# A transformer block with adaptive layer norm and routed experts: batch normalisation of six batches moved from ScalarE to GpSimd, clearing of Q moved from GpSimd to ScalarE, modulation rows spread out

## The reference, cut to what matters

```
mod = silu(c) @ wmod                      # sa, ca, ga, sb, cb, gb for each batch
ga, gb = sign * max(|.|, 0.25)
h = layernorm(x) * (1 + ca) + sa
x = x + ga * attention(h)                 # softmax over 512 keys, 16 heads, 8 batches
h = layernorm(x) * (1 + cb) + sb
x = x + gb * experts(h)                   # top 2 of 8 experts by router logits, gelu between two layers
```

## Time and profile before

| | us |
|---|---|
| median of 3 runs | 657.2 (657.08 to 659.72) |
| the profiled execution's own time | 659.18 |
| its span, first to last instruction | 657.3 |
| front, up to the first maximum on DVE | 52.6 |
| opening, up to the first exponential | 77.3 |
| loop, up to the last exponential | 466.4 |

### The profile page before, as it was taken

The page is one execution under the profiler, slowest core; times in us unless marked ns, Lnnn a source line. Parts: engine busy times, 40 slices in busy tenths (PEclk is TensorE's granted clock), DMA queues, the critical chain, the costliest instruction groups (busy, mean ns, idle before and its releaser), DMA issues.

```text
span 657.3 us, 18907 instructions
## 1 busy us (share of the span) xinstructions
PE 571.7 (87%) x6699; PEld 309.7 (47%) x6699; DVE 499.3 (76%) x1134; ACT 435.2 (66%) x767; POOL 326.2 (50%) x566
## 2 busy tenths in 40 slices
PE   2667999999999999999999999997899687799970
PEld 2321243343443343343343343342589686799970
DVE  4777999989788788788788788787657375565597
ACT  2552488888778788778778778777744353456771
POOL 4444101034456656656656665655065546455571
PEclk9787999999999999999999999999998898899995
DMA  7872400220210310211210220101232122232545
GB/s 199 305 230 91 120 8 11 52 51 11 73 30 25 81 38 26 79 37 26 73 44 24 59 62 19 33 11 38 48 84 58 53 58 75 66 84 70 167 149 168
DMA packets 49867, 48.23 MB, mean 73 GB/s; under 512 B 15616, under 2 KB 44336, under 8 KB 49056
## 3 DMA queue, kind: packets, MB, share of 16 engines
q1 hardware_dynamic: 42256, 36.27, 20.5%
q0 software_dynamic: 4320, 8.92, 4.3%
q10 hardware_dynamic: 3200, 1.84, 1.0%
HBM read 28.77 MB, written 16.53 MB: 69 GB/s over the span
## 4 chain that ended last, share of the span: by engine, by line
PE 67%; DVE 16%; issue 5%; ACT 4%; another core or an unknown queue 3%; POOL 1%; DMA 1%; DVEq 0%; POOLq 0%; SPq 0%; ACTq 0%
PE ps L1018 16%; PE ps L1059 15%; PE ps L1049 13%; DVE neg_max L1363 10%; PE ps L1127 8%; PE ps L1138 7%; ACT P L1226 2%; PE ps L1086 1%; DVE P L275 1%; PE ps L1101 1%; ACT parts L1282 1%; PE ps L1037 1%; DVE ln_stats L259 1%; PE ps L1118 1%
## 5 line engine op out<-in xcount | busy, mean ns | idle before, releaser
L1363 DVE TENSOR_REDUCE neg_max<-ps 128x1 f32<-128x512 f32 x512 | 320.3, 683 | 65.3 <-PE ps L1018 60.4
L1226 ACT ACTIVATE P<-ps,zero 128x1024 f32<-128x1024 f32 x256 | 272.8, 1112 | 80.4 <-PE ps L1049 79.9
L1018 PE MATMUL ps<-K,Q 128*32 128x512 bf16 x2048 | 186.9, 385 | 7.1 <-DVE neg_max L1363 5.0
L1049 PE MATMUL ps<-Q,K 128*32 128x512 bf16 x2048 | 155.4, 380 | 8.6 <-issue 5.2
L1059 PE MATMUL ps<-P,V 128*32 128x512 f32 x1024 | 133.1, 594 | 1.6 <-ACT P L1226 1.4
L1018 PEld LDWEIGHTS ps<-K,Q 128*32 128x32 bf16 x2048 | 54.0, 95 | 127.3 <-DVE neg_max L1363 78.7
L1575 POOL DMA_INDIRECT y_rows<-P,to_now x71 | 70.9, 999 | 86.0 <-DVE P L1415 51.8
L1282 ACT ACTIVATE parts<-ps,parts 128x128 f32<-128x128 f32 x228 | 64.0, 379 | 60.6 <-PE ps L1127 26.7
L1049 PEld LDWEIGHTS ps<-Q,K 128*32 128x32 bf16 x2048 | 50.7, 96 | 74.1 <-issue 34.2
L773 POOL DMA_INDIRECT h_sorted<-diag,slot x64 | 64.4, 1007 | 28.6 <-POOL max_parts L79 13.4
L1127 PE MATMUL ps<-parts 128*128 128x128 f32 x456 | 64.7, 285 | 8.4 <-issue 6.7
(11 more groups left out here) (231 smaller groups left out, 602.2 us busy)
## 6 DMA issues: line engine op xcount, KB each, us to landing
Q<-q_parts SPq DMA_DIRECT2D x24, 384.0 KB
xs<-h_sorted SPq DMA_DIRECT2D x71, 65.0 KB
W<-w_t SPq DMA_DIRECT2D x2, 2048.0 KB, 10.9
q_parts<-parts SPq DMA_DIRECT2D x8, 384.0 KB, 3.0
Q<-y_rows SPq DMA_DIRECT2D x6, 512.0 KB, 4.5
diag<-att_u SPq DMA_DIRECT2D x128, 16.0 KB
Q<-max_parts SPq DMA_DIRECT2D x96, 4.0 KB
out<-Q SPq DMA_DIRECT2D x6, 256.0 KB, 2.3
```

Of the source, the lines that this page charges most:

```text
L1018: ins = eng.matmul(ring_bank(*unit)[QUAD * q:QUAD * (q + 1), :], Q[buffer_of(g)][:, g % NG * G + j, at:at + QUAD], K[buffer_of(g)][:, 0, : ...
L1049: ins = eng.matmul(bank(2 * u + j)[QUAD * q:QUAD * (q + 1), :], K[p][:, 1, at:at + QUAD], Q[p][:, g % NG * G + 2 * u + j, :], start=True, ...
L1226: nc.scalar.activation(P[s % 2][:, 2 * u:2 * u + 2, :], bank(2 * u, 2).rearrange("p (j t) -> p j t", j=2), ACT.Exp, bias=zero[:], scale=SC ...
L1363: eng.tensor_reduce(neg_max[g % 2][:, j * T + s:j * T + s + 1], ring_bank("maximum", g, s, j), AX.X, ALU.max, negate=True).then_inc(ring_u ...
```

## The change

1. `normalize_rows` on ACT goes. `normalized`, four `tensor_scalar` on POOL, stands behind `newton_root` in the group before (n = 2), for batches 0 to 5. Batches 6 and 7 stay on DVE.
2. On POOL `route(…, 1)` moves behind `rows`, next to `route(…, 2)`; `route(…, 3)` stays ahead of `top_two`.
3. ACT clears Q[0] (behind its first activation) and Q[1] (behind its part of the front), each in two Copy activations of 128x2048 words; POOL's two memsets go, and the wait between them.
4. The modulation rows stand after every third unit from unit 5 on; ACT reads out the first maxima after four of them instead of before all.

```diff
 def prepare_gpsimd(eng):
     for operand in (rw, K[0], K[1]):
         eng.memset(operand[:].bitcast(I32), 0).then_inc(op_set, 1)
-    eng.wait_ge(silu_done, START + 1)
-    eng.memset(Q[0][:].bitcast(I32), 0).then_inc(op_set, 1)
...
         normalize(eng, b, xn_done, ON_POOL)
-    eng.memset(Q[1][:].bitcast(I32), 0).then_inc(op_set, 1)
...
 def prepare_scalar(eng):
+    def clear(p):
+        for half in halves_of(Q[p]):
+            nc.scalar.activation(half, zero[:].to_broadcast(list(half.shape)), ACT.Copy).then_inc(cleared, 1)
...
     nc.scalar.activation(silu_den[:], cT[:], ACT.Exp, bias=zero[:], scale=-1.0).then_inc(silu_exp, 1)
+    clear(0)
...
+    clear(1)
...
+def normalized(eng, b):
+    eng.wait_ge(rstd2_own, START + (b + 1) * NEWTON_OPS)
+    if b >= 2:
+        eng.wait_ge(rows_own, START + (b - 1) * ROWS_OPS)
+    for n in range(b * T, (b + 1) * T):
+        eng.tensor_scalar(xn2[b % 2][:, n - b * T, :], X[:, n, :], rstd2[:, n:n + 1], shift2[:, n:n + 1],
+                          ALU.mult, ALU.add).then_inc(xn2_done, 1)
...
-                        b = g * (G * T) + n - 12
-                        if b >= 0 and b % 2 == 0 and b // 2 < B:
-                            modulation_row(b // 2)
+                        b = g * (G * T) + n - 5
+                        if b >= 0 and b % 3 == 0 and b // 3 < B:
+                            modulation_row(b // 3)
...
-                maxima_out(0)
                 for b in range(B):
+                    if b == 4:
+                        maxima_out(0)
...
-                            if s == 0 and u == 1 and batch_at(g, 3) in IN_LOOP:
-                                normalize_rows(batch_at(g, 3), (0, 1))
-                            if s == 1 and u == 0 and batch_at(g, 3) in IN_LOOP:
-                                normalize_rows(batch_at(g, 3), (2, 3))
...
                     if batch_at(g, 2) in IN_LOOP:
                         variance(eng, batch_at(g, 2))
                         newton_root(eng, batch_at(g, 2))
-                    if batch_at(g, 7) in EARLY:
-                        route(eng, batch_at(g, 7), 1)
+                        normalized(eng, batch_at(g, 2))
                     if batch_at(g, 3) in IN_LOOP:
                         rows(eng, batch_at(g, 3))
                     if batch_at(g, 7) in EARLY:
+                        route(eng, batch_at(g, 7), 1)
                         route(eng, batch_at(g, 7), 2)
```

29 lines of the change are left out of this document (9 added, 20 removed).

## The result

| | before | changed |
|---|---|---|
| median of 16 runs each, us | 659.02 (655.4 to 662.47) | 654.92 (652.99 to 657.78) |
| ratio, with its 95% interval | | 0.9944 [0.9928, 0.9961] |
| span of the profiled execution | 657.3 | 653.6 |
| first maximum on DVE | 52.59 | 48.24 |
| first exponential on ACT | 77.32 | 71.85 |

The change is faster by 2.6 to 4.7 us (0.4 to 0.7%), not by 8.6. The forecast had the direction right and the size wrong; 654.9 lies above the range of 644.0 to 653.2. A part of that is the starting point: the forecast stood on 657.2, the median of three runs, and sixteen gave 659.02. In the gain, 4.1 us by the medians, the change fell short of 8.6 by more than half. The two profiled executions differ by 3.64 us, and I follow that number through the stages.

The account below looks back on a forecast made before the run. PE bounds the loop's plain groups, DVE paces the opening, POOL's memset stalls the front. 4.9 - 0.2 + 1.4 + 5.0 - 2.5 = 8.6 us off the 657.2 median gives 648.6; own range 646 to 651.5, whole range 644.0 to 653.2.

Parts of the forecast that it names:

- front: Front: without POOL's memset of Q[1] the 7.88 us step becomes 2.93; gain taken as 4.9 us.
- clearing of Q[0]: Ahead of ACT's copy of mod_T: idle time hides the clearing but for 0 to 0.7 us; 0.2 taken.
- opening: Opening: spread modulation rows cut DVE's waits for PE; gain 1.4 us with one slow row, ends -1.8 and +3.0.
- normalisation: Loop: PE no longer waits behind ACT's normalisation, 0.84 us in each of six groups, 5.0 us gained.
- scatters: Groups 11, 15, 19, 23, 27: scatter stalls take back 0.5 us each, 2.5 in all; ends 0 and 6.5.
- the gain moves to the scatters: Rival, loop: four scatters in a row stall ACT each time, costing 6.5 us instead of 2.5, so 652.6; 15%.
- the wait for a store that I had as a rival: Rival, front: a store or batch 0's load hides the gain, 1 us instead of 4.9, so 652.5; 8%.
- the rival of a POOL that shuts DVE's maxima out: Rival, loop: POOL's new instructions hold up DVE's maxima, 2.5 us in six groups, 15 us, so 663.6; 4%.
- All known costs at their worst: Whole kernel: the worst ends of all terms together give -0.5 us, or 657.7.

Follow-up runs that it names:

- e8: The changed kernel with the normalisation of the first six batches back on ACT, on a free chip: 621.1 us, ratio 0.9908 to the kernel before.
- e5: The changed kernel itself, run again on a free chip: 615.15 us, ratio 0.9806 to the kernel before.
- e1: The kernel before with only the clearing of Q[0] and Q[1] moved to ACT, on a free chip: 622.7 us, ratio 0.9934.
- e13: The changed kernel with one pair of scatters in each of four groups, on a stalled chip: 653.07 us, ratio 0.9910 to the kernel before.
- e3: The kernel before with only the normalisation moved to POOL, second scatter pair still ahead of the rows, on a free chip: 630.2 us, ratio 1.0055.
- e4: The changed kernel with only the second scatter pair put back ahead of the rows, on a free chip: 624.2 us, ratio 0.9955 to the kernel before.
- e16: The changed kernel itself, run a third time, on a stalled chip: 654.98 us, ratio 0.9943 to the kernel before.
- e12: The changed kernel with scatters and plain DMAs added in plain 10.78 us groups, stalled chip: two scatters in a row 11.88 us, four 14.41, plain DMAs 10.78.
- e7: The changed kernel with two or four scatters and plain DMAs added in plain groups, on a free chip: those groups stay at 10.78 us.
- e15: The changed kernel with scatters added singly, spaced by POOL sums, or four narrow in a row, stalled chip: groups of 10.94, 10.91 (two), 11.49 (four), 14.05 us.
- e9: The changed kernel with group 10's scatter pair moved ahead of group 12's, likewise for each early batch, on a stalled chip: 665.9 us, ratio 1.0105 to before.
- e6: The changed kernel with the first four batches' scatters a group later, the fifth's eight together in group 28, on a free chip: 635.5 us, ratio 1.0126 to before.
- e2: The kernel before with only the modulation rows spread, on a free chip: 627.0 us, ratio 1.0015.
- e14: The changed kernel with a batch's eight scatters one by one, other POOL work between them, on a stalled chip: 645.03 us, ratio 0.9796 to before.

## Why the prediction was wrong, step by step

| term | forecast | measured |
|---|---|---|
| front | +4.9 (3.5 to 4.95) | +4.35 in the pair of traces; +5.5 as the mean of sixteen traces with the clearing on ACT (48.4) against four without (54.0) |
| clearing of Q[0] | -0.2 | 0.0 |
| opening | +1.4 (-1.8 to +3.0) | +1.12; +1.2 as a mean |
| normalisation | +5.0, 6 x 0.84 | +5.6, 6 x 0.94 (group 7 here; e8 against e5) |
| scatters | -2.5 (-6.5 to 0) | -6.4 on stalled chips (groups 10 to 28), 0 on free ones |
| not forecast: clock in group 30 | 0 | -1.6 in this pair |
| the rest of the trace | 0 | +0.5 |

**The step that failed is the fifth, the price of the scatters.** I took 0.5 us for each of five groups. In groups 10 to 28 the scatters cost 239.1 - 230.8 = 8.3 us before and 240.8 - 226.1 = 14.7 in the changed kernel, where 230.8 (e1) and 226.1 (e5) are the same groups with no stall. That is 6.4 more, and 5.9 of it lie in groups 11, 15, 19, 23 and 27, 1.2 each: the high end that I had given 15%, as the rival "the gain moves to the scatters". The 3.9 us between 2.5 and 6.4 are most of the 5.0 us by which the traces' 3.6 falls short of 8.6; group 30 is most of the rest. That rival's time of 652.6 stands on the median of 657.2. On 659.02 the same gain gives 654.4, against the measured 654.9.

The mechanism was right, four in a row stall ACT, and its low end is true of another chip. What I misjudged is the price between the ends. I placed the price "nearer to the measured pair than to the four", as if it grew with the number of scatters. It grows faster: 0.16, 1.10 and 3.63 us for one, two and four in a row in plain groups. The loop bears it out: with one pair and no wait for ACT (e13) groups 11 to 27 are 0.4 to 1.2 us over 11.56, with four in a row (the changed kernel) 1.6 to 2.0. The row with "four in a row at 1.99" was the one of the same kind as the change, and I set it aside for one with another count.

**The rest of the steps held.** The front's long step became 2.93 us, and the wait for a store that I had as a rival came once, for 0.65. That the clearing held the front is shown by e1, but I read the wrong instruction as the held one. Two rows of DVE before, the first beside the memset of Q[0] (9.25 to 12.77), the second beside that of Q[1]:

```profile
11.38 1.42 DVE L164 TENSOR_SCALAR ln_mean<-ln_mean 128x8 f32<-128x8 f32 x1
...
36.62 4.04 DVE L275 TENSOR_SCALAR P<-X,ln_mean,ln_rstd 128x128 f32<-128x128 f32 x2
```

Each time it is a `tensor_scalar` that ends with the memset. Of the two at 36.62 one takes 0.34 us and the other 3.79, and the subtractions of the earlier trace rows are behind it in DVE's queue and end at the same moment. Beside the first memset eight statistics of 0.28 us and two `tensor_tensor` of 0.17 run as elsewhere. So the 3.54 us don't show that a subtraction is held, nor that any other DVE instruction would be, and the rival of a POOL that shuts DVE's maxima out had less behind it than I thought.

The rows in the opening cost what I said, with the clock as I said: the first rows slow, then full speed. Group 7 lasts 11.56 where I said 11.7. On POOL I costed four normalising instructions by the front's 0.93 each; in the loop they take 0.45 each, so there was even more room than I counted. The slower rival, POOL shutting DVE out, did not come: the three maxima beside them in group 11 take 0.69 us each, and the mean of all 512 is 0.68. That the pair of scatters must leave the rows' path I costed at nothing; e3 and e4 show that without it the normalisation on POOL gives nothing, since PE then waits 1.5 to 1.8 us for the rows.

**Group 30.** The granted clock is 0.50 for 3.4 us in group 30 of the changed kernel (11.97 us) and of e16 (11.94), not in that of e12 (10.38), whose program is the same there; in group 31 of e5 (13.42), not of e7 (12.04). In the changed kernel PE was busy for 1.33 of the 4 us ahead of it. So the 1.6 us are not fixed to the program. Whether the change makes them likelier these traces can't tell: with e15 (10.71) the dip is in group 30 of three executions of four, and in neither of the two of before. It comes in other groups as well where PE has just waited long (group 11 of e4, 12 and 28 of e9, 14, 18, 22, 26 and 29 of e6), so a wait of PE can cost more than its own length.

**The range.** All known costs at their worst gave 657.7; I cut the range at 653.2 because each rival took only one term to its end. The result took one term to its end and added a clock dip. It also started 1.8 us higher: on 659.02 the upper end is 655.0, at which the measured 654.9 just lies. So the price of the scatters spoiled the forecast, and price, dip and starting point together carried it out of the range.

## What to carry to other kernels

Price a queue of like instructions by how they stand, not only by how many there are. (That the buffers between two engines hide the first delay and expose those that follow before they have refilled fits the 0.16, 1.10 and 3.63 us; no run shows it by itself.) If POOL issues indirect DMAs beside a tight pipeline, put other POOL work between any two of them, but none ahead of something that PE or DVE is about to need. When a move makes one input early, look for the next-late input on the engine that it moved to, and clear the way there in the same change. And time a change on more than one chip: the same program's gain here was 0.6% twice on stalled chips (the result and e16) and 1.9% on a free one (e5).

## What was unexpected of the hardware

- The same program takes 626 to 627 us on two chips and 658 to 660 on three, at the same durations of its instructions: a scatter takes 1.0 us on POOL on both, a plain group 10.78 us. The difference is 22 us in the experts' stage and some 10 in the loop. (The kernel before has no trace on a free chip; this goes by those of e1 and e2.) What differs between the chips no run shows.
- On the three chips work of ACT and DVE that waits for PE starts up to 3.8 us (changed kernel) and 4.4 us (e12) after the end that the trace gives for PE's matmuls: some 50 such starts over 0.35 us in the changed kernel's loop, 1 on a free chip (e5), some 10 in e14. Many of the longest waits are put down to "remote". Whether PE is late itself or its signals arrive late can't be told, since PE's ends are modelled. The Trainium skill, "SBUF — State Buffer", section "Who interferes with whom", says that PE and ACT never wait on anyone for SBUF. These runs don't contradict it: ACT waits here for a signal, and plain DMAs of the same bytes cost nothing.
- The Trainium skill, "Perfetto Trace Analysis", section "DMA Instruction — SWDGE (GPSIMD)", says that the end of such an instruction in a profile is the end of writing descriptors, not of the transfer. With that the 0.8 to 1.3 us from the last scatter's end to ACT's next start would lie inside the transfers. The trace doesn't show these by instruction, so this stays a guess.
- 32 rows in place of 128 shorten a scatter on POOL from 0.96 to 0.86 us, and its price in a row of four, in one group each, from 3.63 to 3.27 us.
- DVE's `tensor_scalar` stood until a memset on POOL ended, for 1.42 and 3.79 us; statistics and `tensor_tensor` beside the same kind of memset did not.
